# Attention projections spread over more PSUM banks, adjacency rows asked for earlier, the first layer norm in quarters

## The reference

```python
h = jnp.maximum(_layernorm(x, axis=-1), 0.0)
x = x + _L0_gnn_ref(h, adj, adj, Wq, Wk, Wv, Wout)   # eight-head attention
h = jnp.maximum(_layernorm(x, axis=-1), 0.0)
x = x + _L1_gnn_ref(h, adj, W1, W2, W3, U1, U2, U3, gamma, beta)
h = jnp.maximum(_layernorm(x, axis=-1), 0.0)
x = x + _L2_gnn_ref(h, adj, W, b)
h = jnp.maximum(_layernorm(x, axis=-1), 0.0)
x = x + _L3_gnn_ref(h, adj, weight)
```

```python
q = (x @ Wq).reshape(h, n, d);  k = (x @ Wk).reshape(h, n, d);  v = (x @ Wv).reshape(h, n, d)
a = jnp.einsum('hnd,hmd->hnm', q, k) * scale
a = a + spatial_encoding + edge_encoding          # both are adj
a = jnp.where(spatial_encoding == 0.0, -1000000.0, a)
a = jnp.where(mask, 0.0, jax.nn.softmax(a, axis=-1))
out = jnp.einsum('hnm,hmd->hnd', a, v).transpose(1, 0, 2).reshape(n, h * d)
return out @ Wout
```

## Time and profile before

| what | value |
|---|---|
| median of 3 runs | 3427.85 us |
| lowest to highest | 3420.27 to 3431.0 us |
| the profiled execution | 3428.46 us, its span 3426.6 us |
| PE, DVE, ACT busy | 2910.1, 2201.0, 1341.7 us |
| setup ends, adjacency ends, attention ends, first refresh ends (from the span's start) | about 57.9, 204, 1964, 2013 us |

### The profile page before, as it was taken

How to read it: one execution, slowest core, us unless ns; L and a number is a source line. 1 busy time by engine, 2 the same in 40 slices (tenths; PEclk the granted TensorE clock), 3 DMA queues, 4 the chain that set the end, 5 groups by cost and what they waited for, 6 DMA issues and landing times. The chain is left out here.

```text
span 3426.6 us, 57642 instructions
## 1 busy us (share of the span) xinstructions
PE 2910.1 (85%) x20376; PEld 2136.8 (62%) x20376; DVE 2201.0 (64%) x4355; ACT 1341.7 (39%) x1734; POOL 58.7 (2%) x68
## 2 busy tenths in 40 slices
PE   2469999999999999999999869778885668687599
PEld 1356676766767667676676537556654466576488
DVE  7965555556565555655656568888687887895430
ACT  4743434334434343443344333323326364632221
POOL 0000000000000000000000000000000000000110
PEclk7579999999999999999999979999987889899799
DMA  7946838468385683865838703010010010100500
GB/s 261 377 152 166 198 89 201 118 169 198 89 198 135 155 200 87 198 150 138 198 90 209 176 31 99 13 38 26 3 56 29 1 43 8 50 22 4 227 1 26
DMA packets 587856, 396.79 MB, mean 116 GB/s; under 512 B 538563, under 2 KB 553414, under 8 KB 562118
## 3 DMA queue, kind: packets, MB, share of 16 engines
q1 hardware_dynamic: 585990, 382.49, 41.4%
q10 hardware_dynamic: 1728, 12.58, 1.1%
HBM read 223.05 MB, written 37.75 MB: 76 GB/s over the span
## 5 line engine op out<-in xcount | busy, mean ns | idle before, releaser
L735 DVE SCALAR_TENSOR_TENSOR e_lo<-e,e_hi 128x2048 f16<-128x2048 f32 x128 | 293.3, 2292 | 441.5 <-ACT e_hi L657 441.5
L597 PE MATMUL av<-vw_hi,pT_hi 128*128 128x256 f16 x2048 | 559.5, 273 | 7.9 <-DMA pT_lo<-e_lo 7.9
L597 PE MATMUL av<-vw_lo,pT_hi 128*128 128x256 f16 x2048 | 559.5, 273 | 0.0
L597 PE MATMUL av<-vw_hi,pT_lo 128*128 128x256 f16 x2048 | 559.4, 273 | 0.0
L586 PE MATMUL logits<-kT_hi,qT_hi 128*128 128x512 f16 x1024 | 389.0, 380 | 9.2 <-DVE att_small L721 7.3
L586 PE MATMUL logits<-kT_lo,qT_hi 128*128 128x512 f16 x1024 | 388.1, 379 | 0.0
L586 PE MATMUL logits<-kT_hi,qT_lo 128*128 128x512 f16 x1024 | 388.1, 379 | 0.0
L651 ACT ACTIVATE att_small<-att_small,minus 128x1 f32<-128x1 f32 x128 | 37.7, 295 | 835.5 <-DVE att_small L730 835.5
L721 DVE CUSTOM_DVE_ANT_0 e<-logits,bias,att_small 128x1024 f32<-128x1024 f32 x256 | 328.6, 1283 | 1.0 <-issue 0.3
L1935 DVE SCALAR_TENSOR_TENSOR nuc_junk<-nuc_e,nuc_thr 128x2048 bf16<-128x2048 f32 x140 | 323.7, 2349 | 6.0 <-issue 2.2
L652 ACT ACTIVATE e<-e,att_small,sc 128x2048 f32<-128x2048 f32 x128 | 266.2, 2079 | 0.0
(11 more groups left out here) (401 smaller groups left out, 5797.6 us busy)
## 6 DMA issues: line engine op xcount, KB each, us to landing
bias<-bias_scratch SPq DMA_DIRECT2D x130, 1024.0 KB, 4.8
bias_scratch<-adj_bias SPq DMA_DIRECT2D x16, 1024.0 KB, 8.1
adjT_scratch<-adjT SPq DMA_DIRECT2D x16, 1024.0 KB, 7.4
nuc_at_hi<-adjT_scratch SPq DMA_DIRECT2D x32, 512.0 KB, 3.7
nuc_at_lo<-adjT_scratch SPq DMA_DIRECT2D x32, 512.0 KB, 4.5
adjT<-adjT_scratch SPq DMA_DIRECT2D x16, 1024.0 KB, 19.9
adj_rows<-in_adj_dram ACTq DMA_DIRECT2D x12, 1024.0 KB, 9.2
adj_rows<-in_adj_dram SPq DMA_DIRECT2D x4, 1024.0 KB, 7.9
```

The costliest lines, as they stand in the source:

```text
L597: last = nc.tensor.matmul(AV[par][:, :], PT[par][w][:, m, :], VW[x][:, m, :], start=(m == 0 and w == x == 0), stop=(m == T - 1 and w == 1))
L735: nc.vector.scalar_tensor_tensor(out=EL[:, :], in0=E[par][:, :], scalar=P_SCALE, in1=EH[:, :], op0=ALU.mult, op1=ALU.subtract).then_inc(lo ...
```

## The change

Five edits.

1. `project(h, 0)`, the K projection: its first two batches go to the two `vw_ps` banks and the other six to the `logits` banks in the order 2, 3, 0, 1, 2, 3. The wait for `logits_read` stands ahead of the third batch. Each batch from the third waits for the count that frees the bank four places back; the first six wait for nothing of this head.
2. `project(h, 3)`, VW: the ring is three banks, `vw_ps0`, `vw_ps1` and `av0`. `av0` and `av1` are now whole banks. Ahead of the third batch stands a wait for `av_free`; ahead of the first head's VW a wait that gamma and beta, which pass through `av0`, have been read.
3. For n = 0 and n = 3 the two rounds are written out on PE, ScalarE and VectorE; Q and V stay loops.
4. The first four adjacency row tiles are asked for in setup, behind Wout and ahead of the second load of `x`; their buffers and semaphores live across both phases.
5. The first refresh works by quads: statistics, `rstd` and its power of -0.5 for four tiles at a time (POOL has four small instructions), VectorE makes `minus` = -mean·rstd (line 1470 of the new kernel), and ScalarE computes Relu(src·rstd + minus) straight from `acc`. `w3` is halved after the first quad's statistics.

```diff
+            with ExitStack() as c1:
+                rows = [sb(c1, f"adj_rows{u}", [P, N]) for u in range(ADJ_AHEAD)]
+                phase(setup, a, bias_d, acc, ident, am, winv, sc, halfp, WH, WL, hT_hi, hT_lo, rows, rows_here)
+                phase(adjacency, a["adj"], bias_d, at_d, sc, ident, deg, row_mask, rows, rows_here)
...
                 sp.dma_start(wo[:, :, :], a["L0_gnn_Wout"].rearrange("(t p) d -> p t d", p=P)).then_inc(w_loaded[3], 16)
+                for u in range(ADJ_AHEAD):
+                    sp.dma_start(adj_rows[u][:, :], adjacency_rows(a["adj"])[u // 2, u % 2, :, :]).then_inc(adj_here[u], 16)
                 sp.wait_ge(extremes, 1)
...
-                for u in range(AHEAD):
-                    sp.dma_start(A[u][:, :], rows[u // 2, u % 2, :, :]).then_inc(loaded[u], 16)
...
-        AV = [ps(c, f"av{n}", [P, D]) for n in range(2)]
+        AVB = [ps(c, f"av{n}", [P, BANK]) for n in range(2)]
+        AV = [AVB[n][:, 0:D] for n in range(2)]
+        EARLY = 2
+        VW_RING = (VP[0], VP[1], AVB[0])
+        GAMMA_BETA_READ = 9
...
-                    with pe.Fori(0, 2) as u:
-                        if n == 0:
-                            pe.wait_ge(logits_read, 32 * h + READS_FREE)
-                        if n == 3:
-                            pe.wait_ge(wo_hi_s, h + 1)
-                            pe.wait_ge(wo_lo_s, h + 2)
+
+                    def half(u):
                         for b in range(4):
                             if kind is None:
-                                pe.wait_ge(vw_free, PER_VW * h + 4 * u + b + 1)
-                                if b == 0:
+                                j = 4 * u + b
+                                if j == 0:
                                     pe.wait_ge(bank_free, KQV * (h + 1) + BANKS_FREE)
+                                if j == 2:
+                                    pe.wait_ge(av_free, T * h - 1 + AV_FREE)
+                                pe.wait_ge(vw_free, PER_VW * h + VW_FREE + max(j - 2, 0))
                                 for m in range(2):
-                                    o = VP[b % 2][:, m * D:(m + 1) * D]
+                                    o = VW_RING[j % 3][:, m * D:(m + 1) * D]
...
-                                pe.wait_ge(bank_free, KQV * h + 8 * n + 4 * u + b + 1)
+                                early = n == 0 and u == 0 and b < EARLY
+                                if n == 0 and u == 0 and b == 0:
+                                    pe.wait_ge(vw_free, PER_VW * h + VW_FREE)
+                                if n == 0 and u == 0 and b == EARLY:
+                                    pe.wait_ge(logits_read, 32 * h + READS_FREE)
+                                if n == 0 and b < EARLY:
+                                    pe.wait_ge(bank_free, KQV * h + BANKS_FREE)
+                                else:
+                                    pe.wait_ge(bank_free, KQV * h + 8 * n + 4 * u + b + 1)
                                 for m in range(2):
-                                    o = bank[b][:, m * ROWS:(m + 1) * ROWS]
+                                    o = (VP[b] if early else bank[b])[:, m * ROWS:(m + 1) * ROWS]
...
+                    if n in (0, 3):
+                        half(0)
+                        half(1)
+                    else:
+                        with pe.Fori(0, 2) as u:
+                            half(u)
...
                 qk(0, 0, 0)
+                pe.wait_ge(vec, GAMMA_BETA_READ)
                 project(0, 3)
...
-                    pl.wait_ge(stats_done, 1)
-                    nc.gpsimd.tensor_tensor(rstd[:, :], rstd[:, :], halfp[:, :], ALU.pow).then_inc(rstd_done, 1)
+                    for b in range(QUADS):
+                        q = slice(QUAD * b, QUAD * (b + 1))
+                        pl.wait_ge(stats_done, b + 1)
+                        nc.gpsimd.tensor_tensor(rstd[:, q], rstd[:, q], halfp[:, q], ALU.pow).then_inc(rstd_done, 1)
...
+                        s.wait_ge(centred, b + 1)
                         for t in range(QUAD * b, QUAD * b + QUAD):
-                            s.wait_ge(centred, t + 1)
-                            nc.scalar.activation(dst[:, t, :], dst[:, t, :], ACT.Relu).then_inc(ready, 1)
+                            nc.scalar.activation(dst[:, t, :], src[:, t, :], ACT.Relu, bias=minus[:, t:t + 1], scale=rstd[:, t:t + 1]).then_inc(ready, 1)
...
+                    stats_of(0)
+                    v.wait_ge(w_loaded, 16 * 5)
+                    nc.vector.tensor_scalar(w3[:, :, :, :], w3[:, :, :, :], 0.5, None, ALU.mult).then_inc(halved, 1)
+                    for b in range(1, QUADS):
+                        stats_of(b)
+                        centre(b - 1)
+                    centre(QUADS - 1)
```

More of the change, by code:

```diff
@@ L50 @@
 P_NUC = 0.9
+ADJ_AHEAD = 4
 G = 4
@@ L144, in build @@
         gb = sb(g, "gamma_beta", [P, 2, D])
+        rows_here = [nc.alloc_semaphore(f"adj_rows_here{u}") for u in range(ADJ_AHEAD)]
         with ExitStack() as c:
@@ L297, in _, with adjacency @@
                     last.then_inc(h_tp, 1)
-def adjacency(nc, sb, ps, sem, adj, bias_d, at_d, sc, ident, deg, row_mask):
-    loaded = [sem(f"adj_loaded{u}") for u in range(4)]
+def adjacency(nc, sb, ps, sem, adj, bias_d, at_d, sc, ident, deg, row_mask, A, loaded):
     (copied, zeroed, made, dve, tposed, hi_done, lo_done, summed) = (
@@ L309, in adjacency @@
     at_stored = [sem(f"at_stored{q}") for q in range(2)]
-    rows = adj.rearrange("(q p c) m -> c q p m", q=2, p=P, c=CH)
-    AHEAD = 4
+    rows = adjacency_rows(adj)
+    AHEAD = ADJ_AHEAD
     HALF = N // 2
     with ExitStack() as c:
-        A = [sb(c, f"adj_rows{u}", [P, N]) for u in range(AHEAD)]
         W = [sb(c, f"adj_permuted{q}", [P, N]) for q in range(2)]
@@ L659, in evacuate, with half @@
                 def evacuate(h, n):
-                    with s.Fori(0, 2) as u:
+                    def half(u):
                         for b in range(4):
@@ L664, in evacuate @@
                             nc.scalar.activation(to[0], source, ACT.Copy, scale=VW_SCALE if n == 3 else 1.0).then_inc(proj_hi, 1)
+                    if n in (0, 3):
+                        half(0)
+                        half(1)
+                    else:
+                        with s.Fori(0, 2) as u:
+                            half(u)
                 def begin(h):
@@ L750, in evacuate, with half @@
                 def evacuate(h, n):
-                    with v.Fori(0, 2) as u:
+                    def half(u):
                         for b in range(4):
```

54 lines of the change are left out of this document (36 added, 18 removed).

## The result

| what | before | after |
|---|---|---|
| median of 4 runs each, same chip | 3427.97 us | 3383.48 us |
| lowest to highest | 3420.27 to 3431.0 us | 3382.86 to 3386.91 us |
| ratio, 95% interval | | 0.9876, 0.9858 to 0.9893 |
| the profiled execution, its span | 3428.46, 3426.6 us | 3382.86, 3381.0 us |

The change saves 44.5 us, 1.3%.

The account below looks back on a forecast made before the run. Attention was taken as bound by PE, adjacency and setup by VectorE, the refresh by a chain. Terms 9.8 + 13.3 + 2.3 + 4.7 + 2.9 = 33.0 us off 3428.46 gave 3395.5 us; 8-in-10 range 3385 to 3408.

Parts of the forecast that it names:

- K projection: Heads two to eight: earlier K start and six banks gain 1.4 us a head, 9.8 us; bounds 0 and 20.
- VW: Heads two to eight: a third bank removes three 0.63 us waits a head, 13.3 us.
- First head: First head's VW: five batches left after the restart, clock falls, gain 2.5 us; net 2.3 us after K's added wait.
- the case that the prediction had weighed and not taken: First head's VW: clock stays up over the shorter 3.7 us idle stretch, ending at 259.5, a gain of 4.5 us.
- Loops written out: K and VW loops: no PE gap at a loop's edge, so costed at nothing, -1 to +1 us.
- The items that follow are bound by PE: Attention items after VW: said to be bound by PE; no gain was priced for them.
- Adjacency: Adjacency phase: rows already in SBUF let ScalarE start sooner, moving the chain by 4.7 us; lower bound 0.
- Rival 2: Setup: Wout slips by the full 3.5 us, total 3399; chance 0.22 shared with rivals 1 and 5 as partial gains.
- First refresh: First refresh: quads start PE 3.1 us earlier, about 2.9 us left as gain; bounds 0 and 4.
- Rival 4: Attention heads: longer PE body needs instruction fetches, 92 us lost, total 3488; chance 0.04.
- Rival 3: First head's clock stays up (2.2 us), K gets three quarters of its bound (5): 3388; chance 0.08 with anything below.
- Rivals 1 and 5: 1: readers fix K's end, DMAs adjacency, 3410; 5: earlier wait blocks seven K starts, 3405; chance 0.22, shared with 2.

Follow-up runs that it names:

- e3: Changed kernel with K's batches back on the four logits banks (EARLY = 0); attention 1729.52 us, 9.1 us more than the changed kernel.
- e1: Kernel before with K and VW loops written out on PE, ScalarE and VectorE, banks and waits unchanged; 3405.36 us, attention 20.8 us less.
- e4: Changed kernel with VW back on two banks, without the av_free wait; attention 1728.58 us, 8.2 us more than the changed kernel.
- e5: Changed kernel with the first refresh as it was before; 3384.41 us in total, 46.53 us from first statistics to the nucleus.
- e6: Changed kernel with one GpSimd multiplication that waits for nothing ahead of the refresh's first power; 46.01 us from first statistics to the nucleus.
- e10: Kernel before with only ScalarE's and VectorE's K and VW loops written out; attention 1743.78 us, 14.5 us less than before.
- e11: Changed kernel with one small GpSimd multiplication near the end of the attention; 43.19 us from first statistics to the nucleus, 2.95 us less.
- e7: Changed kernel with 64 throw-away PE transposes at the refresh's start; 43.77 us from first statistics to the nucleus, 2.4 us less.

## Why the prediction was right or wrong

- **K projection, 9.8 us: right.** Seven starts without a wait, a new wait of 1.35 us (forecast some 1.5) ahead of the seventh batch, put down to `kT_lo`. e3 measures 9.1 us for this part alone.
- **VW, 13.3 us: the waits went whole, but the third bank did only half of it.** VW takes 10.48 us a head instead of 12.43, 1.95 less, forecast 1.9. By e1 and e4 the written-out code alone takes each wait from 0.63 to 0.26, and the third bank the remaining 0.26. The prediction priced the waits and not who makes them. And its price was right by luck: the 15.2 us of the earlier trace rows hold 5.9 of the first head, so that a later head's wait is 9.3 / 21 = 0.44 us in brackets; that average came out at 0.63, which is what such a wait costs from start to start. e4 gives the bank 8.2 us with the first head in it, where the prediction's two terms together say 15.6.
- **First head, 2.3 us: right for the profiled execution, and that the clock fell in it is partly luck.** The second `qk` behind VW came 3.6 us sooner counted from K; VW took 15.73 us, 18.15 without the third bank (e4, 2.4 less) and 18.84 before. What is over the forecast is at least in part the loops'. But in e5 and e6, with the same code here and the same 3.41 us of idleness, the granted clock stayed at 1.00 and VW took 14.06: the case that the prediction had weighed and not taken. Of the eight traces with three banks six have the fall.
- **Loops written out, 0 us: this is the step that failed.** It says "No PE gap stood at a loop's edge, so I cost it at nothing". The cost isn't at the edge. It stands at every wait of the body, on all three engines, and together it is 20.8 us of the attention, of which some 7.6 (7 x 3 x 0.36) are in the sum under VW's name. The other 13 are the forecast's shortfall. The rows that show it stood ahead of the prediction: `ISA` ahead of every batch in the `order` of before and none in that of after. The wait ahead of the `qk` after VW, which was to stay at [0.70], fell to [0.44] for the same reason.
- **"The items that follow are bound by PE": wrong by a little.** An item takes 10.59 us before and 10.55 after, PE comes late to its first `qk` matmul by 0.17 us on average before and 0.12 after, and what shortened that was on the readers' side (e10).
- **Adjacency, 4.7 us: right**, 4.8. Wout landed 25.3 us from its issue (25.2 before) and its reduction didn't move, so the queue served in order here, and DVE set the phase's length. Rival 2 falls.
- **First refresh, 2.9 us: mis-sized, about 1.** The chain was worked out as if POOL were ready; the row 1973.95 had it 7.05 us behind the first statistics, which in the old order is also about when the sixteen statistics and `rstd` were done (6.9 us), so two causes stood at one place and I saw only one. The step that failed is the start of the first power: worked out as free once the quad's statistics were there (1.9 us in), it started 7.4 us in, behind a pair of `MODIFY_POOL_CONFIG`; with the pair out of the way (e11) it started 2.1 us in. And PE's clock, half until 1941.4, took 0.7 us of what was left.
- **Rival 4 falls.** The page of after has 72 packets on q8 and 66 on q14, before 71 and 67; from 490 to 1895 us there is one on q8, as in the earlier trace rows. The longer body costs no fetch here.
- **Rival 3** gave nearly the right time (3388) for the wrong reasons: neither did the clock stay up in the profiled execution, nor K reach its bound.
- **Rivals 1 and 5 fall.** K's end was not fixed by its readers (e3: 1.4 us a head), adjacency gave its 4.8, and the seven starts are free of `logits_read`.
- The remaining 2.3 us are the stretch from the nucleus on, whose scatter is larger than that.

## What to carry to other kernels

Where engines hand a buffer around a short ring, look in the instruction order at how each waits: in this kernel a wait that is an instruction of its own cost 0.11 to 0.15 us at every hand-over, and writing out two loops of two rounds was worth more than three PSUM banks. When two causes could have ended a wait at the same moment, price the step as if the other one stayed; a single instruction that waits for nothing, placed ahead, tells them apart. A gain does not prove the reason that was given for it: e11's was there, and its own trace spoke against the sleep. The listing of a line with the sequencer's instructions showed what the timeline leaves out. And where a wait moves from one engine's queue to the next, the readers' order is the next thing to change: it gave 11 us here without any more memory.

## What the runs showed of the hardware

- GpSimd's first `TENSOR_TENSOR` behind a pair of `MODIFY_POOL_CONFIG`, which comes between a `PARTITION_ALL_REDUCE` and the next `TENSOR_TENSOR`, started 6.97 to 8.55 us behind the pair (40 cases, at the starts of phases), 7.33 us for one that waits for nothing (e6). At the first refresh that was 7.04 to 7.41 us behind VectorE's first statistics (twelve traces), in the later phase that normalises again 7.4 (3136.76 against 3129.33, after). Idleness alone cost nothing there: without the pair just before it, a multiplication after 1648 us started 0.10 us behind its releaser (e11).
- A semaphore wait of its own in a hardware loop: VectorE 0.18 us from ScalarE's end to its start against 0.03, PE 0.17 against 0.06, ScalarE 0.41 behind the start of PE's last matmul against 0.30.
- In the first head of after, PE's granted clock was 1.00 for the first matmuls behind 3.41 us of idleness and then 0.50 for 3.4 us; in e5 and e6, behind the same 3.41 us, it stayed at 1.00. Before, behind 4.95 us, it was 0.50 from the first. Waits of up to 1.7 us left it at 1.00. In the refresh it was back at 1.00 3.1 (e3) to 6.3 us (after) behind the first transpose, and under 9 us of unbroken throw-away transposes (e7) 3.7 us behind the first of them.
- Unchanged code of 1410 us varied by 11 us from one kernel's execution to another's; a part is the clock: the 288 matmuls at the start of the last phase took 31.60 us in after, at 1.00 throughout, and 34.51 before, with 6.0 us of them at 0.50.
